# Attention on paired 64-row halves: masks, scores and maxima as 64-row products, tile-wise maxima five quarters ahead, four heads on two zero-interleaved copies

## The chip, the cores and the metric

One core of a Trainium2 chip. The metric is the device time of one execution in microseconds, lower is better. A comparison comes as a ratio of medians with a 95% interval.

## What is computed

A network of four blocks over x of shape (16, 256, 128) in f32, each with a residual and a layer norm ahead of it: a long convolution, a mixture of experts, attention, and the same mixture of experts again.

```
x = x + conv(norm(x))
x = x + ffn(norm(x))       # 8 experts, top 2, and a shared one, hidden width 512
x = x + attention(norm(x)) # 16 heads of width 8, 256 positions, ALiBi, causal
x = x + ffn(norm(x))       # the same weights
```

The attention is `softmax(q k^T / sqrt(8) + slope_h * (j - i), masked to j <= i) v`, then a product with Wout. The change lies in this block alone, and in the routing of the second expert block that is interleaved with it.

## The kernel before, in words

`build` runs four stages, one after the other, with a barrier between: `front_stage` (convolution, shared expert, routing of the first expert block), `attention_stage`, `shared_stage` (shared expert, rest of the routing of the second block) and `last_stage` (its routed experts, output). `attention_stage` (from L1662) begins with the routed experts of the first block (`routed_program`) and their sum and norm in five pieces (`middle_program`), then does attention batch by batch: 16 batches of 256 tokens, two tiles of 128 tokens each, and the 16 heads as four quarters `G` of four heads `g`.

Precision is made by splitting: a value is an f16 high part and an f16 low part. `project` (L1820) multiplies by the q and k weights, `highs` (L2002, ACT) and `split` (L2095, DVE) form the two parts, `store_qk` (L2008, three DMAs on ACT's queue) writes them to DRAM, and `load_qk` (L1758, five DMAs on SP's queue) brings them back as `KST` (128 rows: part, dimension, head of the quarter) and `QPAD`, in which head g has its values in rows g, g+4, ... and zeros in the others, so that a 128-row product with `KST` yields one head.

A batch has two halves of work, each once a quarter:

- `maxima` (L1838): the scores once with queries in the partitions, so that `reduce` (L2101, DVE, L2109) can take each query's maximum. Three blocks of 512 columns a quarter go alternately to banks 2 and 3; each begins with a product that adds the causal mask (L1845, L1851), then come the heads' products (L1847, L1855). Block n waits until block n-2 is reduced. After two quarters `split_maxima` (DVE), `turn_maxima` (PE, L1863), `maxima_rows` (ACT, L2026) and `spread_m` (L1767, four DMAs on SP's queue) put the negative maxima in two rows of `QPAD`, so that the next product subtracts them.
- `scores` (L1867): the scores again with keys in the partitions, into banks 5 to 7: three mask products (L1876, L1879) and three real ones (L1877, L1880). `expo` (L2028, ACT, L2031) takes the exponential of all 1536 columns at once; `weigh` (L1883, PE, L1894 and L1895) multiplies by v and a column of ones, in four tiles of 32 columns.

The rest of a batch: `take_out` (ACT, L2035), `turn_back` (PE, L1906), `normalise` (DVE, L2123 and L2125), `turn_out` (L1912), `out_high` and `out_low` (ACT L2040, DVE L2136), `project_out` (L1920), `add` (DVE, L2140), `statistics` (DVE, L2131). The norm ahead of the last block follows at once (`batch_norm_program`): `gpsimd` (POOL, L1050 to L1063), `scalar` (ACT, L1070), `turn` (two transposing DMAs on SP's queue, L1079). Three groups of four batches are also routed here: `gate` and `rank` on PE, `logits`, `largest`, `second`, `chosen`, `positions`, `place` on DVE, and the dispatch of two groups, eight tiles at a time, on POOL (L999, L1012).

Every engine runs an order written out by hand: in iteration b the maxima of batch b+1 (`first`), the scores and weighing of batch b (`second`), the projection of batch b+2 and the output of batch b-1, `for G in range(HG)`. On PE a quarter reads:

```
scores(b, q, G)
maxima(b + 1, 1 - q, G, (0, 1))
project(b + 2)              # G == 0
maxima(b + 1, 1 - q, G, (2,))
turn_back / turn_out / project_out of b - 1
weigh(b, q, G)              # waits for this quarter's exponential
values(b + 1)               # G == 3
```

## Time and profile before

| | |
|---|---|
| Median of 3 runs | 952.41 us (949.72 to 954.01) |
| Profiled execution | 951.15 us, its span 949.3 us |
| PE busy | 671.7 us, 71% of the span |
| PE weight loads | 491.6 us, 52% |
| DVE busy | 646.1 us, 68% |
| ACT busy | 445.5 us, 47% |
| POOL busy | 460.9 us, 49% |
| Mean granted TensorE clock | 0.890 of full speed |

The span runs from the first to the last instruction; the execution's own time is a little longer. An engine's busy time leaves out its waits and its register, branch, semaphore and DMA-issuing work. Products on PE are pipelined, so that records overlap: the distance from start to start tells more than a duration. The attention proper lies between about 407 and 735 us; the routed experts before and behind it have limits of their own. A wait is counted for the engine that stood idle and given to what ended it. SPq is SP's queue of DMA issues, ACTq that of ACT, PEld the weight loads.

### The profile page before, as it was taken

What the parts mean: (1) busy time and instruction counts of PE and PEld (TensorE: products, weight loads), DVE (VectorE), ACT (ScalarE), POOL (GpSimd) and SP (SyncE); (2) the same over time, 40 slices, a digit from 0 to 9 for tenths busy, and PEclk for the clock granted to TensorE, in tenths of its full rate; (3) what the DMA queues carried; (4) which work ended last, traced back from release to release, by engine and by line L of the source; (5) the groups of instructions that cost most, each with busy time, mean ns of one, the idle gap of its engine ahead of it and who ended that gap; (6) DMA issues with size and microseconds to landing.
All of it is one profiled execution on the core that took longest, in us unless ns stands there. A gap on an engine that the chain in (4) does not pass through costs nothing. (4 is left out here: it accounts for less than half of the span.)

```text
span 949.3 us, 21195 instructions
## 1 busy us (share of the span) xinstructions
PE 671.7 (71%) x7378; PEld 491.6 (52%) x7378; DVE 646.1 (68%) x1459; ACT 445.5 (47%) x873; POOL 460.9 (49%) x569
## 2 busy tenths in 40 slices
PE   0278964860099997157988988888983785999960
PEld 0163433650089996034555655555552464899850
DVE  6989987760278886685666676576661673788865
ACT  6632366730055554355455555455542431555534
POOL 2037758887537777110111226316421784477770
PEclk9978997985589999568999999999997897999995
DMA  9410002241444542521122223213300141454417
GB/s 288 109 35 1 0 7 70 66 88 52 40 73 91 98 92 44 199 57 41 41 66 63 55 63 86 80 52 90 86 8 12 43 80 31 81 96 93 96 32 265
DMA packets 137507, 70.45 MB, mean 74 GB/s; under 512 B 89237, under 2 KB 126619, under 8 KB 137400
## 3 DMA queue, kind: packets, MB, share of 16 engines
q1 hardware_dynamic: 113646, 44.16, 20.7%
q0 software_dynamic: 9088, 16.88, 6.1%
q10 hardware_dynamic: 14672, 8.06, 3.1%
q8 instruction: 64, 1.05, 0.5%
q14 instruction: 37, 0.30, 0.1%
HBM read 26.61 MB, written 30.50 MB: 60 GB/s over the span
## 5 line engine op out<-in xcount | busy, mean ns | idle before, releaser
L2109 DVE TENSOR_REDUCE ARENA<-banks 128x2 f32<-128x512 f32 (+1 forms) x192 | 126.8, 687 | 88.2 <-PE banks L1847 85.7
L1432 ACT ACTIVATE ARENA<-banks,ARENA 128x256 f32<-128x256 f32 x312 | 122.1, 475 | 109.7 <-PE banks L1395 97.6
L1393 PE MATMUL banks<-ARENA,W1H 128*128 128x256 f16 x312 | 87.2, 279 | 69.0 <-DMA ARENA<-slots 62.1
L2031 ACT ACTIVATE ARENA<-banks 128x1536 f32<-128x1536 f32 x64 | 92.0, 1437 | 58.7 <-PE banks L1880 58.7
L1407 PE MATMUL banks<-W2L,ARENA 128*128 x624 | 110.6, 219 | 2.7 <-DVE ARENA L1445 2.3
L1408 PE MATMUL banks<-W2H,ARENA 128*128 x624 | 110.0, 219 | 0.1
L1409 PE MATMUL banks<-W2H,ARENA 128*128 x624 | 110.1, 219 | 0.0
L1383 POOL DMA_INDIRECT expert_out_g<-ARENA x78 | 80.6, 1033 | 47.7 <-issue 25.8
L1383 POOL DMA_INDIRECT expert_out_f<-ARENA x78 | 81.3, 1043 | 39.0 <-issue 25.6
L1466 DVE TENSOR_TENSOR ARENA<-ARENA 128x1024 f16<-128x1024 f32 x78 | 95.6, 1226 | 2.7
L999 POOL DMA_INDIRECT slots<-ARENA,PLACE x64 | 77.3, 1208 | 26.1 <-issue 18.1
L1394 PE MATMUL banks<-ARENA,W1H 128*128 128x256 f16 x312 | 87.1, 279 | 0.0
L1395 PE MATMUL banks<-ARENA,W1L 128*128 128x256 f16 x312 | 87.0, 279 | 0.0
L1012 POOL DMA_INDIRECT slots<-ARENA,PLACE x64 | 77.5, 1210 | 19.1 <-issue 14.6
L1464 DVE CAST ARENA<-ARENA 128x1024 f16<-128x1024 f32 x78 | 58.2, 746 | 38.8 <-ACT ARENA L1432 34.2
L1393 PEld LDWEIGHTS banks<-ARENA,W1H 128*128 x312 | 31.2, 100 | 74.5 <-issue 70.9
L479 PE MATMUL banks<-XN,ARENA 128*128 128x512 f32 x64 | 32.2, 661 | 47.0 <-ACT XN L398 40.8
L1407 PEld LDWEIGHTS banks<-W2L,ARENA 128*128 128x128 f16 x624 | 60.9, 98 | 5.0 <-issue 3.9
L1408 PEld LDWEIGHTS banks<-W2H,ARENA 128*128 128x128 f16 x624 | 60.9, 98 | 1.6 <-issue 0.3
L1409 PEld LDWEIGHTS banks<-W2H,ARENA 128*128 128x128 f16 x624 | 61.0, 98 | 0.0
L1050 POOL TENSOR_TENSOR NRM<-RSTATS 128x2 f32<-128x2 f32 x15 | 3.1, 203 | 116.3 <-DVE RSTATS L2131 116.2
L1851 PE MATMUL banks<-ARENA 128*128 128x256 bf16 x128 | 36.3, 283 | 28.2 <-DVE ARENA L2109 28.0
(318 smaller groups left out, 1897.8 us busy)
## 6 DMA issues: line engine op xcount, KB each, us to landing
spread<-ARENA ACTq DMA_DIRECT2D x48, 128.0 KB, 2.0
ARENA<-expert_out_f SPq DMA_DIRECT2D x8, 512.0 KB, 7.2
ARENA<-spread SPq DMA_DIRECT2D x16, 256.0 KB
ARENA<-spread SPq DMA_DIRECT2D x64, 64.0 KB
ARENA<-expert_out_g SPq DMA_DIRECT2D x8, 512.0 KB, 7.2
XT<-in_w SPq DMA_DIRECT2D x10, 256.0 KB, 7.6
slots<-EMPTY SPq DMA_DIRECT2D x16, 129.0 KB, 4.7
ARENA<-in_w SPq DMA_DIRECT2D x8, 256.0 KB, 6.9
```

The costliest lines, as they stand in the source:

```text
L1012: nc.gpsimd.indirect_dma_start(xs, bass.IndirectOffsetOnAxis(ap=t.PLACE[:, 1, i:i + 1], axis=0), ROWI[:, i, :], None).then_inc(sent[h], 16)
L1383: nc.gpsimd.indirect_dma_start(yo, bass.IndirectOffsetOnAxis(ap=target, axis=0), Y[i % 4][:, h], None, bounds_check=2 * NT * P - 1, oob_is ...
L1393: pe.matmul(out, t.W1H[:, e, ms], XST[i][:, 0], start=True, stop=False)
L1394: pe.matmul(out, t.W1H[:, e, ms], XST[i][:, 1], start=False, stop=False)
L1395: ins = pe.matmul(out, t.W1L[:, e, ms], XST[i][:, 0], start=False, stop=True)
L1407: pe.matmul(out, hh, t.W2L[:, e, m, :], start=(m == 0), stop=False)
L1408: pe.matmul(out, hh, t.W2H[:, e, m, :], start=False, stop=False)
L1409: ins = pe.matmul(out, hl, t.W2H[:, e, m, :], start=False, stop=(m == MT - 1))
L1432: ins = nc.scalar.activation(HF[i % 2][:, m], UP[i % 2][:, m], ACT.Gelu, bias=BIAS[i % 4][:, m:m + 1], scale=1.0 / WS)
L1466: dve.tensor_tensor(H16[i % 4][:, 1], HF[i % 2], H16[i % 4][:, 0], ALU.subtract).then_inc(split, 1)
L2031: nc.scalar.activation(PR[G % 2], t.psum_all[:, 5:8, :], ACT.Exp, scale=1.0 / LOGIT).then_inc(exps, 1)
L2109: dve.tensor_reduce(out, src, AX.X, ALU.max).then_inc(m_red, 1)
```

## The change

All in `attention_stage` and `batch_norm_program`, with the layout of two host tables.

- Layout. The four heads of a quarter become two halves `a` of 64 partitions with two heads `s` each. `KST` keeps 128 rows, ordered half, dimension, part, head. `QPAD` has two copies `s` instead of four `g`: copy s has its heads' rows in every second partition and zeros between. A head's product now uses the 64 partitions of its half, in `KST` and `QPAD` alike.
- Masks. Instead of a 128-row identity times a mask there is a shifted identity `SPREAD` of 64 rows in each half and two masks, `LATER` and `EARLIER`; each mask is made by two products, one of the full 128 columns a head and one of 64.
- `maxima(y, tile)`: two calls a quarter, one for each query tile, half a into bank 2+a: mask products of 256 and 128 columns in each half, then for both heads 128 columns (tile 0) or 256 (tile 1), 16 products a quarter for 15. `reduce(y, tile)` takes both banks at once: 512 elements (tile 0) or 1024 (tile 1). Tile 0 is done four quarters ahead of the scores, tile 1 five.
- `scores(x)`: 12 products for 6, alternating between the halves; three semaphore steps instead of one, the middle of it with a wait, because half 1 writes to bank 7 after half 0.
- Order on PE: `maxima(x + 4, 0)`, `scores(x)`, `maxima(x + 5, 1)`, the batch's other work, and `weigh(x - 1)`, the weighing of the quarter before.
- The batch's other work moves: projection three batches ahead, output two batches behind, values into bank 0 at G = 2; turning back at G = 2 and 3, turning out at G = 0 and projecting out at G = 1 of the next iteration.
- DMAs. The stores of q and k go from ACT's queue (three) to SP's (six); the loads are three instead of five, and the maxima's rows two for each half batch instead of four. SP waits for batch b-3's rows between the two `spread_m` of batch b+1.
- Norm and routing. POOL's `gpsimd` is cut into `statistics(c)` and `rows(c)`, and the rows come one batch later, behind the next batch's statistics; ACT's part is one iteration later, gate and rank two iterations later, at G = 2; POOL dispatches four tiles at a time.
- The loops run from b = -2 to 17 instead of -1 to 16, and PE does `project(0)` ahead of them.

The diff, cut to its core:

```diff
-        QPAD = [carve(F16, HG, GH, SEQ) for _ in range(3)]
+        QPAD = [carve(F16, 2, HG, SEQ) for _ in range(3)]
         V32 = [carve(F32, TPB, NH, 32) for _ in range(2)]
-        IDB, MASKB, MASKT = carve(BF16, P), carve(BF16, GH, P), carve(BF16, GH, P)
+        SPREAD = carve(BF16, 2 * P)
+        LATER, EARLIER = carve(BF16, 2, P + HALF), carve(BF16, 2, 2 * P)
...
+            for b in range(-3, NB + 2):
+                if batch(b + 2):
                     load_qk(b + 2)
-            body(-2, 0, STAGES[-2])
-            pipeline(sp, body)
+                if batch(b + 3):
+                    store_qk(b + 3)
+                if batch(b + 1):
+                    spread_m(b + 1, 0)
+                if 0 <= b - 3 < NB - 1:
+                    batches.turn(sp, b - 3)
...
+                batches.statistics(pool, c)
+                if c >= 1:
+                    batches.rows(pool, c - 1)
+                for g in range(SENT_IN_ATTENTION):
+                    piece = c - 4 * g - 6
+                    if piece in (0, 1):
+                        route.dispatch_first(pool, g, range(GRP // 2 * piece, GRP // 2 * piece + GRP // 2))
+                    if piece in (2, 3):
+                        route.dispatch_second(pool, g, (piece - 2,))
...
+            def mask_later(out, a, part, start):
+                first, n = ((HALF + HALF * a, HALF), (HALF * a, P))[part]
+                rows = SPREAD[PAIR[a], first:first + P]
+                pe.matmul(out, rows, LATER[PAIR[a], :, first:first + n], start=start, stop=False, skip_group_check=True)
...
+            def maxima(y, tile):
+                c, G = divmod(y, HG)
+                if G == 0 and tile == 1:
+                    pe.wait_ge(qk_in[c % 3], 48 * (c // 3 + 1))
+                after(pe, m_red, 2 * y + 1 - tile)
+                keys, queries = P * tile + P, slice(P * tile, P * tile + P)
+                out = [ps[2 + a][:, 0:2 * keys].rearrange("p (s n) -> p s n", n=keys) for a in range(2)]
+                for a in range(2):
+                    mask_earlier(out[a][:, :, P * tile:P * tile + P], a, 0, True)
+                for a in range(2):
+                    mask_earlier(out[a][:, :, P * tile + HALF:P * tile + P], a, 1, False)
+                for s in range(2):
+                    for a in range(2):
+                        ins = pe.matmul(out[a][:, s], QPAD[c % 3][PAIR[a], s, G, queries], KST[c % 3][PAIR[a], G, 0:keys],
+                                        start=False, stop=True, skip_group_check=True)
+                        if s == 1:
+                            ins.then_inc(m_mm, 1)
...
+            def scores(x):
+                c, G = divmod(x, HG)
                 if G % 2 == 0:
-                    after(pe, mrow_in[G // 2], 64 * b + 64)
-                if b == 0 and G == 0:
...
+                after(pe, exps, x)
...
+                mask_later(late[0], 0, 1, True)
+                mask_later(early[1], 1, 1, True)
+                mask_later(late[0][:, :, 0:HALF], 0, 0, False)
+                mask_later(early[1][:, :, 0:HALF], 1, 0, False)
+                late_scores(0).then_inc(st_mm, 1)
+                early_scores(1)
+                mask_later(early[0], 0, 1, True)
+                mask_later(early[0][:, :, 0:HALF], 0, 0, False)
+                pe.wait_ge(st_mm, 3 * x + 1)
+                mask_later(late[1], 1, 1, True)
+                early_scores(0).then_inc(st_mm, 1)
+                mask_later(late[1][:, :, 0:HALF], 1, 0, False)
+                late_scores(1).then_inc(st_mm, 1)
...
+            def quarter_of(b, G):
+                x = HG * b + G
+                if quarter(x + 4):
+                    maxima(x + 4, 0)
+                if quarter(x):
+                    scores(x)
+                if quarter(x + 5):
+                    maxima(x + 5, 1)
+                if G == 0:
+                    if batch(b + 3):
+                        project(b + 3)
+                    if batch(b - 2):
+                        turn_out(b - 2)
...
+                if quarter(x - 1):
+                    weigh(x - 1)
...
+            def reduce(y, tile):
+                c, G = divmod(y, HG)
+                dve.wait_ge(m_mm, 4 * y + 4 - 2 * tile)
+                keys = P * tile + P
+                src = t.psum_all[:, 2:4, 0:2 * keys].rearrange("p a (s n) -> p a s n", n=keys)
+                dve.tensor_reduce(MX[:, G // 2, tile, :, :, G % 2].rearrange("p s a -> p a s"), src, AX.X, ALU.max).then_inc(m_red, 1)
...
+            def quarter_of(b, G):
+                x = HG * b + G
+                if quarter(x + 4):
+                    reduce(x + 4, 0)
+                    if G % 2 == 1:
+                        split_maxima(b + 1, G // 2)
+                if G == 1 and batch(b - 2):
+                    out_low(b - 2)
+                if quarter(x + 5):
+                    reduce(x + 5, 1)
+                if G == 0:
+                    if batch(b + 3):
+                        split(b + 3)
+                    if rank_group(b) is not None:
+                        route.second(dve, rank_group(b))
+                if G == 1:
+                    if batch(b - 2):
+                        add(b - 2)
+                    if rank_group(b) is not None:
+                        route.chosen(dve, rank_group(b))
+                if G == 2:
+                    if batch(b - 1):
+                        normalise(b - 1, 0)
+                    if batch(b - 2):
+                        statistics(b - 2)
+                    if gate_group(b) is not None:
                         route.logits(dve, gate_group(b), ps[0])
...
```

## Rows read from the trace of the kernel before

**Rows 1.** The exponential's line: durations, first and last start in us.
```profile
L2031 ACT ACTIVATE ARENA<-banks x64: 1422/1450/1452, 429.0 to 718.2; 128x1536 f32<-128x1536 f32 x64
```

**Rows 2.** Stretches of the attention stage: PE, PEld, DVE, ACT, POOL busy (x), clock.
```profile
400.00:429.00 29.00, 15.48 (x96) 9.89 (x97) 23.22 (x71) 15.05 (x42) 3.27 (x2) 0.62 0.23 63
...
521.50:540.00 18.50, 16.45 (x195) 10.56 (x188) 11.65 (x27) 9.52 (x13) 3.67 (x13) 1.00 0.24 66
540.00:558.40 18.40, 16.34 (x208) 10.64 (x201) 13.91 (x39) 9.51 (x13) 3.66 (x13) 1.00 0.23 63
```

**Rows 3.** Waits from 429 to 718: us in total, times, longest.
```profile
DVE ARENA L2109 <- PE banks L1847: 84.8, 57, 3.2
...
ACT ARENA L2031 <- PE banks L1880: 56.8, 32, 2.6
...
PE banks L1851 <- DVE ARENA L2109: 22.4, 46, 1.8
```

**Rows 4.** Timeline of PE in one quarter: start, us, instruction, wait ahead.
```profile
545.66 0.28 PE L1876 MATMUL banks<-ARENA 128*128 128x256 bf16 x1
...
547.20 0.27 PE L1851 MATMUL banks<-ARENA 128*128 128x256 bf16 x1
...
548.24 0.28 PE L1851 MATMUL banks<-ARENA 128*128 128x256 bf16 x1 [0.55 <-DVE ARENA L2109]
...
548.58 0.60 PE L1906 MATMUL banks<-ID,ARENA 128*128 128x128 f32 x4
549.12 0.66 PE L1894 MATMUL banks<-ARENA 128*32 128x256 f32 x8
549.57 0.42 PE L1895 MATMUL banks<-ARENA 128*32 128x128 f32 x8
549.93 0.28 PE L1876 MATMUL banks<-ARENA 128*128 128x256 bf16 x1
```

**Rows 5.** Groups by form, 429 to 718: busy us and mean ns behind the bar.
```profile
L2109 DVE TENSOR_REDUCE ARENA<-banks 128x2 f32<-128x512 f32 x120 | 82.3, 686 | 0.9 <-PE banks L1855 0.3
L1855 PE MATMUL banks<-ARENA 128*128 128x128 f16 x480 | 46.6, 220 | 0.0
L1877 PE MATMUL banks<-ARENA 128*128 128x512 f16 x126 | 44.9, 383 | 0.0
```

**Rows 6.** Timeline of the gate's weight loads, three to a token tile.
```profile
540.28 0.12 PEld L928 LDWEIGHTS banks<-GWH,XT 128*128 128x128 f16 x2
...
540.35 0.12 PEld L928 LDWEIGHTS banks<-GWH,XT 128*128 128x128 f16 x2
```

**Rows 7.** Timeline ahead of the first exponential, at 429.0.
```profile
402.27 2.62 SPq L1764 DMA_DIRECT2D ARENA<-spread  x4
...
406.71 0.59 PE L1845 MATMUL banks<-ARENA 128*128 128x512 bf16 x1 [4.26 <-DMA ARENA<-spread]
...
410.74 0.57 ACT L2005 ACTIVATE ARENA<-banks 128x512 f16<-128x512 f32 x1
...
422.85 1.23 DVE L1598 TENSOR_TENSOR RES<-RES,ARENA 128x1024 f32<-128x1024 f32 x1
```

**Rows 8.** Timeline of SP's queue over one batch.
```profile
568.80 2.50 SPq L1079 DMA_TRANSPOSE XT<-ARENA  x2
571.34 2.55 SPq L1770 DMA_DIRECT2D ARENA<-ARENA  x4
...
587.29 2.58 SPq L1079 DMA_TRANSPOSE XT<-ARENA  x2
```

**Rows 9.** Timeline behind the last exponential, batch 14's rows.
```profile
714.46 12.97 SPq L1079 DMA_TRANSPOSE XT<-ARENA  x4
...
719.62 0.20 POOL L1050 TENSOR_TENSOR NRM<-RSTATS 128x2 f32<-128x2 f32 x1 [5.23 <-DVE RSTATS L2131]
...
722.82 0.88 ACT L1070 ACTIVATE XN<-RES,NRM 128x128 f32<-128x128 f32 x2 [1.55 <-POOL NRM L1060]
...
724.25 0.65 POOL L1063 TENSOR_TENSOR ARENA<-XN,ARENA 128x256 f16<-128x256 f32 x1
```

More of the change, by code:

```diff
@@ L66 @@
 BACK_WORDS = 2 * NT * D
+HALF = P // 2
 class Bag:
@@ L1083, in landed @@
         eng.wait_ge(turned[(c - first) % 4], 16 * TPB * ((c - first) // 4 + 1))
-    part.gpsimd, part.scalar, part.turn, part.landed = gpsimd, scalar, turn, landed
+    part.statistics, part.rows, part.scalar, part.turn, part.landed = statistics, rows, scalar, turn, landed
     return part
@@ L1711, in attention_stage @@
         ps = t.psum
+        PAIR = [slice(HALF * a, HALF * a + HALF) for a in range(2)]
+        MAX_ROW = 30
+        LAST = HG * NB
         (consts_in, cleared, masks, cast, m_high, rc_set) = (sem(n) for n in (
@@ L1723, in after @@
         def after(eng, s, n):
-            if not (isinstance(n, int) and n <= 0):
+            if n > 0:
                 eng.wait_ge(s, n)
@@ L1754, in _, with store_qk @@
             sp.wait_ge(cleared, 8)
+            def store_qk(c):
+                after(sp, qk_in[c % 3], 48 * (c // 3))
+                sp.wait_ge(parts, c + 1)
+                words = DENSE[c % 2].rearrange("p k n -> p (k n)").bitcast(F32).rearrange("p (k n) -> p k n", k=4)
+                for i, kinds in enumerate(((1, 2), (1, 3), (0, 2))):
+                    for k in range(2):
+                        to = t.dram["spread"][c % 3][k][:, :, :, i].rearrange("s a d G n -> (s a d) G n")
+                        sp.dma_start(to, words[:, kinds[k]]).then_inc(dense_out[c % 2], 16)
@@ L1763, in load_qk @@
-                for g in range(GH):
-                    sp.dma_start(QPAD[c % 3][g:P:GH, :, g, :].bitcast(F32), q[g]).then_inc(qk_in[c % 3], 16)
-            def spread_m(c, r, h):
-                after(sp, mrow_set, 2 * c + h + 1)
-                for g in range(GH):
-                    row = GH * 26 + g
-                    sp.dma_start(QPAD[c % 3][row:row + GH + 1:GH, 2 * h:2 * h + 2, g, :],
-                                 MROW[h][4 * g:4 * g + 4, :]).then_inc(mrow_in[h], 16)
-            def body(b, q, stages):
-                second, first, projections, output = stages
-                if second:
-                    spread_m(b, q, 1)
-                if 2 <= b <= NB:
-                    sp.wait_ge(v_mm, b - 1)
-                    batches.turn(sp, b - 2)
-                if first:
-                    spread_m(b + 1, 1 - q, 0)
-                if projections:
-                    load_qk(b + 2)
@@ L1820, in project @@
             def project(c):
-                if c < TPB:
-                    pe.wait_ge(middle.low, 1)
+                if c <= 2 * TPB:
+                    pe.wait_ge(middle.low, c // TPB + 1 if c < 2 * TPB else NG)
+                after(pe, parts, c)
+                after(pe, mrow_set, 2 * (c - 2))
                 for k in range(2):
@@ L1972, in body @@
                         route.rank(pe, rank_group(b), ps[0])
-                    if b == 0:
-                        middle.turn(pe, 4 + G)
-                    if first and G == HG - 1:
-                        after(pe, added, b)
-                        if b == 0:
-                            pe.wait_ge(middle.low, NG)
-                        values(b + 1)
+                if G == 3:
+                    if batch(b + 1):
+                        after(pe, vset, b + 2)
+                        if gate_group(b) is not None:
+                            route.logits_taken(pe, gate_group(b))
+                        if rank_group(b) is not None:
+                            route.ranks_taken(pe, rank_group(b))
+                        turn_maxima(b + 1, 1)
+                    if batch(b - 1):
+                        turn_back(b - 1, 1)
@@ L1988, in _ @@
+            for b in range(-2, NB + 2):
+                for G in range(HG):
+                    quarter_of(b, G)
         @block.scalar
@@ L2077, in _ @@
             middle.normal(act, 2)
-            pipeline(act, body)
+            for b in range(-2, NB + 2):
+                for G in range(HG):
+                    quarter_of(b, G)
         @block.vector
@@ L2194, in _ @@
             middle.add(dve, 3)
-            pipeline(dve, body)
+            for b in range(-2, NB + 2):
+                for G in range(HG):
+                    quarter_of(b, G)
 def host_tables():
```

460 lines of the change are left out of this document (198 added, 262 removed).

## The prediction

> **What bounds the kernel now.** I read the stretches of the attention stage first, then the exponential's own rows, the waits, one quarter of a batch on PE, and last the two ends of the stage. From the first exponential (429.0) to the last (718.2) there are 63 intervals in 289.2 us [rows 1]; two batches' transposes on SP are 18.49 us apart, so a full quarter (one group G of one batch) takes 4.62 us [rows 8]. In such a batch PE is busy 16.4 of 18.5 us, DVE 11.7 to 13.9, ACT 9.5 [rows 2]. DVE's idle time ends with the first product of maxima, ACT's with the last product of scores; PE itself waits for one thing of weight, DVE's maxima, before it may write a bank again [rows 3]. So PE in program order is the bound, with a stall inside.
>
> A quarter on PE, start to start [rows 4]: scores and maxima block 0 1.54 (3584 columns at 2.4 per ns are 1.49), block 1 with the stall 1.04 (0.32 of it work, 0.72 stall), block 2 0.34, turning back 0.54 (0.44 plus 0.10 until the weighing starts), weighing 0.81. Without the batch's own work this is 3.90 with 0.17 for the drain ahead of the weighing: 1.54+1.04+0.34+0.17+0.81. The batch's own work is, by columns, project 0.64, turn out 0.22, two turned maxima 0.44, project out 0.32, turning back 0.88, values 0.32: 2.8 us. Four quarters plus that: 15.6+2.8 = 18.4 against 18.49 measured. The accounting holds, so I use it for the changed kernel.
>
> **Columns.** A 512-column product takes 383 ns and a 128-column one 220 ns [rows 5]: 384 columns in 163 ns, 2.4 columns per ns, plus 0.17 us until the result is there. Masks, scores and maxima stream 5120 columns a quarter now: 2.13 us. After: tile 0 of the maxima has 640 columns in each 64-row half, tile 1 has 896, the scores 1536. If the two halves run side by side that is 3072 columns, 1.28 us, and offsets in the scores (1640 by the order written) make it 1.32. The number of weight loads rises from 21 to 28 a quarter; load and 8-column product together follow at 25 ns here (three of each in 0.07 us) [rows 6], so 28 loads are 0.7 us and stay covered by the columns.
>
> Whether 64-row halves overlap no row shows. The nearest is the weighing, where four tiles of 32 columns take turns: eight products of 256 columns start within 0.45 us (549.12 to 549.57) [rows 4], where one after another they would need 0.85. Full overlap is one bound (1.32), none the other (6144 columns, 2.56 us). I take full overlap with 0.1 us lost, since that row is the nearest and shows tiles of one array overlapping.
> Going from the whole array to the 32-column tiles and back costs PE about 0.17 us before the weighing (its first product waits until the last result is out) and 0.20 behind it, the latter inside the 0.81 [rows 4]. The stretch of halves adds one such change a quarter, priced at the same 0.17 us; bounds 0 and 0.3.
> The Trainium skill ("TensorEngine Tiling (Array Packing)", Tiling Modes) has both rules: two 64x128 tiles load and multiply in parallel, and a change of tiling mode drains the engine. The trace agrees on the drain, with those 0.17 and 0.20 us; of 64-row tiles it shows nothing.
>
> **DVE.** Three reductions of 512 elements at 0.686 us [rows 5] become one of 512 and one of 1024; a 1024-element operation takes 1.23 us [rows 7]. 2.06 becomes 1.92 us a quarter. The new order decides more: maxima tile 0 is issued first, its reduction runs from 0.48 to 1.17 us in the quarter while the scores stream to 0.95, so the second maxima start at 1.22 instead of waiting 0.72. A stall of about 0.25 stays. Before, weighing waited for its own quarter's exponential; now it is the previous one's, which is done at 2.6 us.
>
> **The new quarter:** to the end of the second maxima 1.59 (1.22+0.37), switch 0.17, own work 0.71, drain 0.17, weighing 0.81: 3.45. With maxima turned behind DVE (0.2 in two quarters of four) 3.5 us; ACT (2.5 us of work) and DVE (about 3.0) fit beside it. I add 0.1 for pairs that do not line up and 0.1 for DVE's and ACT's fixed orders: **3.7 us**. 59 full quarters (all but the last four): 218.3 against 272.6 now.
>
> **Routing.** Three times, gate and ranking now stand at G=2 behind the values' evacuation (ACT does it after that quarter's exponential, so it is ready at about 3.1 us, and PE is there at 2.6), and largest, second and place are DVE work of 2.3 us a batch (13.91 against 11.65) [rows 2], which is free today. With DVE at 90% it isn't: I price 4 us a group, **12 us**, bounds 0 and 16.
>
> **The last four quarters** have no maxima: scores 0.68, switch 0.17, own work 0.71, drain 0.17, weighing 0.81, with waits 2.8 us each, 11.2 together, against 289.2-272.6 = 16.6 now.
> Stage between the exponentials: 218.3+12+11.2 = 241.5 against 289.2, **-47.7**.
>
> **Fill, +8.** Today the first maxima start at 406.7, ahead of the second projection's evacuation (410.74) [rows 7]; the first exponential at 429.0. Afterwards DVE's split of batch 1, which needs that evacuation, stands ahead of the first reduction in DVE's order, so the first reduction falls from 407.8 to about 412; a chain follows in which each tile's maxima wait for the other tile's reduction, partly at the low clock (0.62 in this stretch [rows 2]). Counted through in DVE's order, with about 0.9 us of PE between two reductions: the first three reductions end at 413.2, 414.8 and 417.1; batch 2's split at 418.4; the statistics of the expert output's fourth piece at 420.9; two reductions, the split maxima and the two low parts at 425.2; two more reductions at 428.2; that piece's weighting and addition (2.2 and 1.23 us) at 431.8; the last two at 434.7; then the scores at 1.2 GHz. First exponential near 437. Bounds +3 and +10.
>
> **Tail, +5.** Batch 14's statistics start POOL's chain at 719.62, at the end of the last exponential (718.2+1.45). POOL takes 3.2 us, ACT's two rows 0.88, POOL's two casts to 724.90, and the transposes' issue goes on to 727.43 (714.46+12.97) [rows 9]. After the change these statistics stand on DVE behind batch 15's first normalisation, which needs weighing (0.9), take-out (0.6) and turning back (0.7) before its own 0.55, all with their hand-overs; with the statistics' 0.5 that is 3.6 us after that exponential's end. POOL's chain ends at 6.9, and batch 13's rows, which moved behind it, at 8.0; batch 14's own follow at 9.2. So four transposes (1.25 us each) queue from 8.0 on: the last issue ends 13.0 us after the exponential instead of 7.8. Bounds +2 and +7.
>
> SP takes over six stores (ACT's three issues, about 0.45 us each, leave ACT), but has two loads and four spreads fewer: some 9 us of issue a batch, within 14. The memsets shrink by about 3 us, under the expert rounds: nothing.
>
> **Sum:** 951.15 - 47.7 + 8 + 5.2 = 916.7. The profiled execution is 1.3 us below the median of 952.41, so **917.5** as a median. A measurement tells about 0.5% (4.8 us) from nothing.
>
> **Rivals.**
> (1) *A chain over SP becomes the bound.* The row statistics of batch b-2, POOL's sums and rows (4.6 us: 719.62 to 724.90 [rows 9], less ACT's 0.88, with a wait), two transposes (2.5), then on the same queue the second half of the maxima's rows (2 of the 0.64 us issues: 2.55 for four [rows 8]) and some 1.8 us of landing (issue over at 404.9, PE off at 406.71 [rows 7]) must be over before the scores of G=2 in the next batch. From those scores to the statistics' end it is 3.9 us by the new quarter's count. The ring is 3.9+4.6+2.5+1.3+1.8, 14.1 us in all, beside PE's 14.0 to 14.8 a batch. For it: everything sits behind SP's wait for rows. Against: 14.1 us is still within four quarters of 3.7. With 1.8 us of contention the quarter is 4.0: 59 x 4.0+12+11 = 259, time 934. Chance 0.20.
> (2) *The stalls I priced do not come:* quarter 3.5, routing 4, fill 4: 206.5+4+11 = 221.5, time 893. Chance 0.12.
> (3) *The halves do not overlap*, so the change does not do what its pairing says. Stretch 2.56 instead of 1.59; the quarter is 2.56+0.17+0.71+0.17+0.81 = 4.4, with waits 4.5: 265.5+4+12.4 = 282, time 951-7+13 = 957: slower. It decides once stretches exceed 2.4 us. For it: twelve score products where there were six, and no 64-row form in the trace. Against: the weighing's overlap. Chance 0.06.
> By the Trainium skill ("TensorE: Matmul & The Clock Gate", Measured speedup vs the span model) four row tiles gave 3.07 times; an estimate at that 77% efficiency makes the stretch's columns 1.67 us, about 0.3 us a quarter above mine, 935 in all; no run here shows it yet.
> (4) *The granted clock falls to 1.2 GHz*, as it stood for part of 400 to 429 [rows 2], since PE waits elsewhere more. The 2.7 us of columns in a quarter double: 59 x 2.6 more, about 1070. Against: at 16.4 of 18.5 us busy it stands at 1.00, and PE would still be busy three quarters of the time; 0.02.
>
> **Numbers.** The forecast has 0.60, its own range 903 to 930. The range holds it, rival 1 and the nearer part of rival 2: 897 to 938. Faster 0.91 (forecast, rivals 1, 2 less a rest), same 0.03, slower 0.06.
>
> **What the profile would show.** Products of form 64*128, two starting within a few ns in different halves; a stretch of about 1.6 us; reductions of 1.22 us for 1024 elements; exponentials 3.6 to 3.8 apart; first exponential near 437; last transpose 13 us behind the last exponential. I am wrong if pairs start one after the other, if exponentials wait for the DMA of maxima rows, or if DVE is busy through and PE waits for it.

## The result, and the profile after

| | before | after |
|---|---|---|
| median of 6 runs, us | 952.07 (949.72 to 954.01) | 901.90 (899.87 to 902.89) |
| profiled execution, us | 951.15, span 949.3 | 901.03, span 899.3 |
| TensorE's granted clock, mean | 0.890 | 0.876 |
| ratio | | 0.9474 (0.9456 to 0.9492) |

The change takes 50 us where 34.5 were forecast. By the marks that the prediction set in the stage, the two spans differ so:

| stretch | before | after | difference | forecast |
|---|---|---|---|---|
| start of the program to start of the attention stage | 250.1 | 250.5 | +0.4 | 0 |
| from there to the experts' first product | 11.2 | 5.7 | -5.5 | 0 |
| from there to the first exponential | 167.7 | 174.2 | +6.5 | +8 |
| first to last exponential | 289.2 | 230.6 | -58.7 | -47.7 |
| last exponential's start to the next stage | 17.3 | 24.6 | +7.3 | +5.2 |
| behind it | 213.8 | 213.8 | 0 | 0 |

The differences sum to -50.0 (each was taken before rounding). The page's head and first part after:

```profile
span 899.3 us, 21979 instructions
PE 633.2 (70%) x7826; PEld 468.5 (52%) x7826; DVE 635.0 (71%) x1395; ACT 445.1 (49%) x873; POOL 456.7 (51%) x569
```

The exponential's line, which answers to [rows 1]:

```profile
L2072 ACT ACTIVATE ARENA<-banks x64: 1422/1450/1452, 430.3 to 660.9; 128x1536 f32<-128x1536 f32 x64
```

The same 64 instructions of 1.45 us, the first 1.4 us later, the last 57.3 earlier. Stretches of the stage, as in [rows 2]:

```profile
445.00:500.00 55.00, 53.20 (x824) 34.95 (x824) 43.20 (x80) 36.40 (x48) 6.77 (x27) 1.00 0.25 70
500.00:560.00 60.00, 54.33 (x857) 36.00 (x857) 46.16 (x100) 37.50 (x52) 14.50 (x53) 1.00 0.27 76
```

PE is the bound as before, at a granted clock of 1.00 (2.4 GHz): 53.2 of 55 us busy in the quiet batches (those without routing). DVE went up to 79% (43.2 of 55). The waits from 430 to 661, against [rows 3]:

```profile
ACT ARENA L2072 <- PE banks L1919: 58.2, 62, 3.2
DVE ARENA L2150 <- PE banks L1891: 40.3, 75, 1.9
PEld banks L1875 <- DVE ARENA L2150: 27.0, 71, 3.6
```

ACT and DVE wait for PE's products. PE's own wait for the maxima is still there, in the smaller form that the prediction left it. The quarter on PE, start to start, against [rows 4]:

```profile
542.82 0.34 PE L1875 MATMUL banks<-ARENA 64*128 64x256 bf16 x4
543.00 0.28 PE L1891 MATMUL banks<-ARENA 64*128 64x128 f16 x4
543.11 0.33 PE L1868 MATMUL banks<-ARENA 64*128 64x256 bf16 x4
...
543.78 0.27 PE L1919 MATMUL banks<-ARENA 64*128 64x256 f16 x1
544.18 0.34 PE L1875 MATMUL banks<-ARENA 64*128 64x256 bf16 x4
544.35 0.40 PE L1891 MATMUL banks<-ARENA 64*128 64x256 f16 x4
544.67 0.28 PE L1899 MATMUL banks<-ID,ARENA 128*16 128x128 f16 x2
544.88 0.65 PE L1960 MATMUL banks<-ID,ARENA 128*128 128x128 f32 x4
545.47 0.66 PE L1948 MATMUL banks<-ARENA 128*32 128x256 f32 x8
545.92 0.42 PE L1949 MATMUL banks<-ARENA 128*32 128x128 f32 x8
546.28 0.34 PE L1875 MATMUL banks<-ARENA 64*128 64x256 bf16 x4
```

Three things are to be seen. The maxima of tile 0, 1280 columns of both halves together (L1875 masks, L1891 products), go from 542.82 to 543.11: 4.4 columns per ns, where the whole array took 2.4 in the kernel before. The scores' 3072 columns follow from 543.11 to 543.89, 0.78 us or 3.9 columns per ns; their last 256-column product starts at 543.78. And the stall that was 0.72 us is now 0.29: from 543.89, 0.11 us behind that start, to tile 1's start at 544.18. The whole quarter is 3.46 us. The reductions, against [rows 5], have the two forms that were priced, at 1.23 and 0.69 us:

```profile
L2150 DVE TENSOR_REDUCE ARENA<-banks 128x4 f32<-128x1024 f32 x59 | 72.3, 1226 | 27.5 <-PE banks L1891 27.5
...
L2150 DVE TENSOR_REDUCE ARENA<-banks 128x4 f32<-128x512 f32 x59 | 40.8, 692 | 14.0 <-PE banks L1891 12.7
```

From the starts of the 64 exponentials: in batch 3 they stand 3.54, 3.27, 3.49 and 3.45 us apart, 13.75 a batch. Before, the shortest batches (1 and 2) had 4.02, 4.66, 3.78 and 4.93, 17.39 in all, and batches 3 and 4 took 17.9. Batch 0 takes 18.5 (24.8). The batches with routing take 15.2, 16.9 and 14.5 (7, 8, 9) and 15.0, 16.9 and 14.1 (11, 12, 13).

### The profile page after: what moved, and what is told of

It reads as the page before. It is cut to its first block and busy times, and to the rows that moved or that the text cites. A ratio compares the mean times of both kernels' runs of the same rounds, so it can differ in the third digit from the quotient of the medians.

```text
span 899.3 us, 21979 instructions
## 1 busy us (share of the span) xinstructions
PE 633.2 (70%) x7826; PEld 468.5 (52%) x7826; DVE 635.0 (71%) x1395; ACT 445.1 (49%) x873; POOL 456.7 (51%) x569
## 5 line engine op out<-in xcount | busy, mean ns | idle before, releaser
L2150 DVE TENSOR_REDUCE ARENA<-banks 128x4 f32<-128x1024 f32 (+1 forms) x128 | 122.7, 959 | 46.7 <-PE banks L1891 45.4
L1388 POOL DMA_INDIRECT expert_out_g<-ARENA x78 | 80.6, 1034 | 47.7 <-issue 25.8
L1875 PE MATMUL banks<-ARENA 64*128 64x256 bf16 (+1 forms) x512 | 45.6, 258 | 32.8 <-DVE ARENA L2150 23.6
```

The source lines that it names most:

```text
L1388: nc.gpsimd.indirect_dma_start(yo, bass.IndirectOffsetOnAxis(ap=target, axis=0), Y[i % 4][:, h], None, bounds_check=2 * NT * P - 1, oob_is ...
L2150: dve.tensor_reduce(MX[:, G // 2, tile, :, :, G % 2].rearrange("p s a -> p a s"), src, AX.X, ALU.max).then_inc(m_red, 1)
```

## Experiments

They ran in four sessions. In two of them the kernel before took 953 us, in the other two 1065 and 1054, one of these on a chip that had given 953 in another session; so each ratio is against the runs of before in its own session, and effects under 1% are read in traces, of which there is one for each kernel. The extra time is not in the quiet quarters, which keep 13.75 and 17.39 us a batch to 0.01 us. Between the exponentials of kernels of the before type it lies in batches 7, 8, 11 and 12, where POOL scatters rows; they go from about 18 to 26 us. That is 32 of the 114 us by which the profiled run with 2 KB rows (below) is longer than that of before. 10 us more lie ahead of the attention stage, 39 in its routed experts ahead of the first exponential, and 33 in the stages behind it. What makes a session long was not found.

### The order of issue: one half behind the other

In each of the three groups half 0's products are all issued ahead of half 1's:

```diff
-                for a in range(2):
-                    mask_earlier(out[a][:, :, P * tile:P * tile + P], a, 0, True)
-                for a in range(2):
-                    mask_earlier(out[a][:, :, P * tile + HALF:P * tile + P], a, 1, False)
-                for s in range(2):
-                    for a in range(2):
+                for a in range(2):
+                    mask_earlier(out[a][:, :, P * tile:P * tile + P], a, 0, True)
+                    mask_earlier(out[a][:, :, P * tile + HALF:P * tile + P], a, 1, False)
+                    for s in range(2):
```

> The changed kernel with the same 28 products a quarter, but all of half 0 issued before all of half 1, so that two halves meet only where one ends and the other begins. Theory P (the halves run side by side and that halves the stretch): the stretch grows from 1.6 to about 2.5 us, a quiet quarter from 3.44 to 4.3, exponentials' span from 230.6 to about 285, time 950 to 960, that is the time before the change. Rival O (the new order and the weighing a quarter late took the stalls away, PE has slack): a quarter grows by under 0.2 us, time under 915.

Measured: 903.9 us, ratio 0.9486 (0.9463 to 0.9509), a quiet batch of 13.88 us. Rival O's number came, but not for its reason: the pairs do not live by their order, and the timeline of PE (tile 0 of a quarter) says why:

```profile
544.42 0.35 PE L1875 MATMUL banks<-ARENA 64*128 64x256 bf16 x4
544.60 0.28 PE L1889 MATMUL banks<-ARENA 64*128 64x128 f16 x4
544.71 0.33 PE L1868 MATMUL banks<-ARENA 64*128 64x256 bf16 x2
```

All four masks start before any product of L1889, although half 0's two products stand in the program ahead of half 1's two masks; and tile 0 still takes 0.29 us (544.42 to 544.71). So products for the other rows of the array start ahead of earlier ones, and here the pairing did not need the order of issue. The run leaves the overlap as it was and so doesn't price it. That took two more.

### The overlap itself: the halves held apart, and its control

The first holds half 1 until half 0 is done, in each of the three groups; the second has as many new waits, behind both halves. In the first, the new wait inside the scores takes the place of the one that stood there.

```diff
                 for a in range(2):
+                    if a == 1:
+                        pe.wait_ge(m_mm, 4 * y + 3 - 2 * tile)
...
                 early_scores(0).then_inc(st_mm, 1)
+                pe.wait_ge(st_mm, 3 * x + 2)
                 mask_later(early[1], 1, 1, True)
```

```diff
                             ins.then_inc(m_mm, 1)
+                pe.wait_ge(m_mm, 4 * y + 4 - 2 * tile)
...
                 late_scores(1).then_inc(st_mm, 1)
+                pe.wait_ge(st_mm, 3 * x + 3)
```

> The kernel after, with the second half's products held back: in each of the three groups of a quarter's stretch (maxima of tile 0, scores, maxima of tile 1) PE waits for a semaphore that half 0's last product raises before it issues half 1's first. Theory P (two 64-row products run side by side, which is what the quarter lives on): the stretch's 6144 columns (1280, 3072 and 1792) then run at one column a cycle, 2.56 us at 2.4 GHz, where side by side they take 1.28; with three waits of some 0.2 us the quiet quarter goes from 3.45 to 5.0 to 5.4 us and the run to 990 to 1015 us. Rival O (the 0.29 us of a tile's starts is how the records come out, and the time is one of handovers): only the waits are paid, the quarter is about 4.0 us and the run about 940, like the run with waits alone.

> The control for the run with the halves held apart: the kernel after, with three waits a quarter as well, but behind both halves of a group (PE waits for the group's last product before it issues what follows), so that the halves still run side by side. Both theories: three waits of some 0.2 us each, a quiet quarter of about 4.0 us and a run of about 940 us. What the run with the halves apart costs above this one is the price of losing the overlap: 1.28 us a quarter, some 55 to 78 us in all, by theory P, under 10 us by rival O.

Measured: 972.4 us, ratio 1.0178 (1.0136 to 1.0219), with the halves apart; 924.5, ratio 0.9694 (0.9669 to 0.9718), with the waits alone. The quiet quarters are 4.55 and 3.84 us (18.18 and 15.37 a batch). So a wait costs 0.13 us on average (0.40 us for three), not 0.2, and holding the halves apart costs 0.70 us a quarter on top. In all that is 48 us: 42 between the exponentials, 5.5 ahead of the first and 1 behind the last. Rival O, which gave it less than 10, fell. Theory P gave 1.28 us a quarter, 55 to 78 in all, and is right in kind but too high. This kernel keeps some overlap between its groups, though how much of the missing 0.58 us that is was not measured. PE with the halves apart:

```profile
500.68 0.28 PE L1875 MATMUL banks<-ARENA 64*128 64x256 bf16 x1
500.74 0.27 PE L1868 MATMUL banks<-ARENA 64*128 64x256 bf16 x1
500.80 0.22 PE L1875 MATMUL banks<-ARENA 64*128 64x128 bf16 x1
500.85 0.21 PE L1868 MATMUL banks<-ARENA 64*128 64x128 bf16 x1
```

Half 1's masks for the scores (L1868) and half 0's for the next group, tile 1 (L1875), start in turns, 0.05 to 0.06 us apart. The 48 us thus price the overlap inside the groups, and are a lower bound for all of it. With 48 us more the changed kernel would stand at 950: an estimate, by which the overlap is worth as much as the whole gain. The parts need not add up, since the new order may gain nothing where the halves are slow; the joined reductions were not tried alone.

### The weighing a quarter later

```diff
-                if quarter(x - 1):
-                    weigh(x - 1)
+                if quarter(x):
+                    weigh(x)
```

with ACT's take-outs one quarter earlier.

> The changed kernel with each quarter's weighing in its own quarter again (as before the change), and the two copies of its result a quarter earlier. Theory W (with PE this fast its own exponential is not done yet): PE reaches the weighing 2.3 to 2.6 us into the quarter and the exponential ends at 2.65, so 0.1 to 0.4 us a quarter, time 909 to 920, and the wait of the weighing for the exponential rises from 1 to over 10 us. Rival S (the batch's own work covers it, as it did before): within 3 us of 902.

Measured: 911.1 us, ratio 0.9567 (0.9544 to 0.9590); a quiet batch of 14.3 to 14.5 us, about 3.6 a quarter. The weighing now waits for its own quarter's exponential:

```profile
500.90 0.66 PE L1948 MATMUL banks<-ARENA 128*32 128x256 f32 x8 [0.16 <-ACT ARENA L2072]
```

Moving the weighing behind by a quarter is worth 9 of the 50 us.

### The second maxima four quarters ahead, not five

```diff
-                if quarter(x + 5):
-                    maxima(x + 5, 1)
+                if quarter(x + 4):
+                    maxima(x + 4, 1)
```

DVE reduces in the same order, so that the split of the maxima (L2159) comes behind the long reduction.

> The changed kernel with both tiles of the maxima four quarters ahead (tile 0, scores, tile 1 of the same quarter), so that the maxima are split behind the long reduction. Theory L (the fifth quarter of lead takes the 1024-element reduction out of the way of PE's turned maxima): PE waits about 1.6 us in G=1 and G=3, a quiet batch grows from 13.75 to about 17 us, time 945 to 955, first exponential 1 to 3 us earlier. Rival N (DVE is not in the way, the lead only costs fill): time 898 to 903.

Measured: 987.7 us, ratio 1.0354 (1.0319 to 1.0389). That is 86 us above the changed kernel and beyond every expectation. The waits from 440 to 720:

```profile
PE banks L1899 <- DVE ARENA L2159: 51.3, 27, 2.3
ACT ARENA L2067 <- PE banks L1899: 39.7, 27, 2.7
```

The turning of the maxima (L1899) stands in the middle of PE's program, and its input is now made behind the long reduction, which itself waits for this quarter's second maxima. PE stands still for 1.9 us in every second quarter, ACT's copy of the turned rows waits behind it, and so do the exponentials. That is 51 of the 86 us, and about what theory L priced. Most of the rest goes with TensorE's granted clock. It is 0.84 over 440 to 560, where the changed kernel has 1.00 from 445 on, and it falls behind most of PE's stands:

```profile
508.29 0.27 PE L1899 MATMUL banks<-ID,ARENA 128*16 128x128 f16 x2 [1.86 <-DVE ARENA L2159]
...
509.53 1.10 PE L1948 MATMUL banks<-ARENA 128*32 128x256 f32 x8
...
511.00 0.50 PE L1875 MATMUL banks<-ARENA 64*128 64x256 bf16 x4
```

From 508.3 to 511.8 the granted clock was 0.52, that is the lower level of 1.2 GHz, and from 511.9 to 518 it was 1.00. The weighing takes 1.47 us start to start (509.53 to 511.00) instead of 0.81. By the trace's clock records there are 23 such stretches from 440 to 720 for 27 stands, 85 us in all. At half speed they cost PE at most 43 us, where 35 us lie beyond the waits; the split is an estimate, and no run held the clock apart from the waits. The fifth quarter of lead keeps DVE's chain out of PE's.

### The start of the stage: four runs

Here 5.5 us came that no term of the sum had. Two things differ there: POOL's clearing is shorter (8.2 us, now 5.6), and the fixed rows are copied in another form. The first run is the changed kernel with its three cleared copies cleared twice:

```diff
+            for v in words:
+                nc.gpsimd.memset(v, 0.0).then_inc(cleared, 1)
+            pool.wait_ge(cleared, 3)
             for v in (*words, V32[0], V32[1], SPREAD, LATER, EARLIER):
```

The others are the kernel before with its copies changed. First they are written as 2 KB rows:

```diff
-                sp.dma_start(t.dram["spread"][r][:, 3], t.dram["fixed_rows"]).then_inc(consts_in, 16)
+                sp.dma_start(t.dram["spread"][r][:, 3].rearrange("k d g G n -> k (d g) (G n)"),
+                             t.dram["fixed_rows"].rearrange("k d g G n -> k (d g) (G n)")).then_inc(consts_in, 16)
```

Then each is split into two that take every other row:

```diff
+                for g in range(2):
+                    sp.dma_start(t.dram["spread"][r][:, 3].rearrange("k d g G n -> k (d g) (G n)")[:, g::2],
+                                 t.dram["fixed_rows"].rearrange("k d g G n -> k (d g) (G n)")[:, g::2]).then_inc(consts_in, 16)
```

Last, the copies are turned so that the 32 rows are outermost:

```diff
+                sp.dma_start(t.dram["spread"][r][:, 3].rearrange("k d g G n -> (d g) k (G n)"),
+                             t.dram["fixed_rows"].rearrange("k d g G n -> (d g) k (G n)")).then_inc(consts_in, 16)
```

> The changed kernel with its three cleared copies cleared twice, so that POOL's clearing is as long as before the change (8.2 instead of 5.6 us) while the constant rows keep their new form. Theory M (POOL's clearing at the stage's start holds up DVE's copies and the first expert): first expert product 3 to 5 us later, time 905 to 907. Rival F (the form of the constant rows did it): 902, DVE's two copies longer but nothing behind them.

> The kernel before the change, with nothing altered but the form of its first three DMAs of the attention stage: the constant rows go as rows of 2 KB (as in the changed kernel) instead of as two stretches of 64 KB. Theory F (the long stretches hold up the DMA engines, and with them the first expert's transposed tile): the first expert product comes at 256 instead of 261.3 us, time about 5 us less, 947. Rival M (POOL's longer clearing holds it up): no change, 952.

> The kernel before, with each of the three copies of the fixed rows split into two that take every other 2 KB row, so that a copy can't be sent as two runs of 64 KB each. Theory R (the long runs hold up the transposes that stand behind them in the queue): the first expert's first product comes about 7.5 us behind the start of the clearing, where it is 11.1 now (5.7 as in the kernel after, and three more issues of 0.6 us), and the run is 3 to 4 us shorter, 948 to 949 on a chip where before takes 952. Rival C (it is the clearing or the placement of something else in that stage that the change altered): 11 to 13 us, and no gain, or 2 us of loss for the three more issues.

> The kernel before, with the same three copies of the fixed rows written with the 32 rows of 2 KB as the outer dimension and q against k inside, where before, and in the run that split them, q against k (two) is outermost. Theory E (a copy is dealt to the DMA engines by its outermost dimension, so that two of them carry all of it, and the transposes' packets stand behind): the copies land within 3 us, the first expert's first product comes 5.5 to 6 us behind the start of the clearing instead of 11.1, and the run is 5 to 5.5 us shorter: ratio 0.994 to 0.995. Rival N (something else of the changed layout, not these copies): 11 us as before and a ratio of 1.000.

Measured, from the start of the clearing to the experts' first product: before 11.2 us; after 5.7; clearing doubled 5.7 (ratio 0.9531, 0.9478 to 0.9584); 2 KB rows 11.1 (1.0016, 0.9967 to 1.0066); every other row 11.1 (0.9991, 0.9977 to 1.0005); rows outermost 5.7 (0.9927, 0.9888 to 0.9966). It is not the clearing, since doubling it changed nothing. Written as 2 KB rows the copies were sent as before: rows that lie next to each other in memory still went as six packets of 64 KB (3219 packets in that run's view, 3213 of them under 8 KB), so that run did not test the length. With every other row 192 packets of 2 KB went, and the first product came no sooner (its three more issues put the transposes back by 1.9 us only), so it is not the length either. The DMA view of the stage's first microseconds (busy tenths of the 16 engines in 40 slices) before, 249 to 262:

```profile
DMA  0000000090000000009999900440000000799992
...
DMA packets 2327, 0.79 MB, mean 61 GB/s; under 512 B 2321, under 2 KB 2321, under 8 KB 2321
```

(The time of a packet counts in the slice in which it starts: the 9 alone in its place is the first two 64 KB packets, of 3.3 to 3.5 us each.)

With every other row in a copy, 249 to 264:

```profile
DMA  0000000011120111111011699971411999912087
```

With the rows outermost, 250 to 270:

```profile
DMA  0000000355730560247025620661183208411008
...
spread<-in_fixed_rows SPq DMA_DIRECT2D x3, 128.0 KB, 2.6
```

With q against k, two, as the outermost dimension and every other row in a copy, a tenth to two tenths of the engines are busy for some 4 us, about two of 16. The packet records say the same: before, two of the six 64 KB packets are under way at a time, and the last ends at 260.06, ahead of the experts' first product at 261.3. With 32 rows outermost up to 19 packets of 2 KB are under way at once, the copies land in 2.6 us, and the transposes behind them in the same queue bring the experts their rows 5.4 us sooner. That the outermost dimension deals a copy out to the engines is the reading that fits all six kernels; no record here names the engine of a packet. The Trainium skill has it as a rule ("DMA: Bandwidth & Descriptors", Why a DMA increments its semaphore by 16 and not by 1): the largest number up to 16 that divides the slowest dimension of both sides, so two engines for the old form and 16 for 32 or 64 rows. The trace agrees, with two packets at a time for the old form, and with 11.1 us against 5.7. The changed layout puts 64 rows outermost, so the 5.5 us come with it by the way, and the kernel before can have them by changing one statement (measured in the long session, 0.7% with an interval of 0.3 to 1.1).

### Routing behind the weighing

In the quarter G = 2 of the changed kernel the gate's products and the ranks' stand ahead of the weighing and wait there for ACT's evacuation of the values (here the gate's):

```profile
541.34 0.19 PE L929 MATMUL banks<-GWH,XT 128*128 128x8 f16 x2 [0.67 <-ACT ARENA L2061]
```

The edit moves both blocks, unchanged, behind `weigh(x - 1)`. It ran in two sessions.

> The changed kernel with gate and rank behind the weighing at G=2 instead of ahead of it. Theory G (PE stands 0.7 us for ACT's copy of the values and then does the gate, with everything behind it late): the long quarters at G=2 of the routing batches (4.9 us) shrink by 0.5 to 1.0 us, six of them, time 897 to 900. Rival D (DVE's routing work sets those quarters): no change, 901 to 903.

> The kernel after, with the gate's products and the ranks' issued behind the quarter's weighing instead of ahead of it, on the chip of the first runs. By the intervals seen on the other chip (the third quarter of a gate's batch 4.18 us instead of 4.91, of a rank's 3.81 instead of 4.36, the batch of the first transposes behind it 14.3 instead of 15.2) it gains 2 to 3 us in all: some 899 us, ratio 0.944 to 0.945. If the routing's cost is all in DVE's work and PE's place doesn't matter: 902, ratio 0.947.

Measured: ratios 0.9460 (0.9407 to 0.9513) and 0.9480 (0.9425 to 0.9534), against 0.9474 for the change. In the intervals the gate's quarter falls from 4.91 to 4.18 us and the ranks' from 4.36 to 3.81, in both sessions. With 0.2 us lost elsewhere in the ranks' batch (16.6 against 16.9) this is 1 us a group, less than both expectations had. The times can't show so little: both sessions were those of the long batches. Most of what is left of the ranks' batch (16.6 against 13.75) is in its first two quarters, 4.7 and 4.6 us, where PE waits for DVE, which then does the routing's arithmetic as well. In the changed kernel it waits 0.95 us at 548.45, and then:

```profile
553.32 0.34 PE L1875 MATMUL banks<-ARENA 64*128 64x256 bf16 x4 [1.37 <-DVE ARENA L2150]
```

### The tail

```diff
-                pool.wait_ge(row_stats, c + 1)
-                batches.statistics(pool, c)
                 if c >= 1:
                     batches.rows(pool, c - 1)
+                pool.wait_ge(row_stats, c + 1)
+                batches.statistics(pool, c)
```

and DVE's statistics of batch b - 2 ahead of the normalisation of b - 1.

> The changed kernel with POOL's rows of batch c-1 ahead of its statistics of batch c again, and DVE's statistics at G=2 ahead of the normalisation. Theory T (the end of the stage is the chain statistics of batch 14, POOL, ACT, POOL, four transposes queued): the last transposes are issued 2 to 4 us earlier after the last exponential, the next stage begins as much earlier, time 898 to 900. Rival B (the barrier or batch 15 sets the end): 901 to 903.

Measured: ratio 0.9466 (0.9421 to 0.9512), and 24.1 us from the last exponential's start to the next stage, against 24.6. DVE's statistics do come sooner (4.7 us behind the exponential's end instead of 6.2), but POOL begins on them 6.8 us behind it, as against 7.0. It now stands at batch 13's row first:

```profile
738.38 0.40 POOL L1067 CAST ARENA<-XN 128x256 f16<-128x256 f32 x1 [2.38 <-ACT XN L1075]
...
739.60 0.20 POOL L1052 TENSOR_TENSOR NRM<-RSTATS 128x2 f32<-128x2 f32 x1
```

What DVE's half of the edit gave, POOL's half mostly took back. Statistics moved alone were not tried.

## Why the prediction was right, and where it was not

The median, 901.9, lies in the range, and 1 us under the low end of the forecast's own, which had the chance of 0.60. The mechanism is the one that was named, and the sizes of five steps were off. From 917.5 to 901.9 are -15.6 us: -11 between the exponentials, -5.5 at the start of the stage, -1.5 in the fill, +2.1 in the tail and 0.4 ahead of the stage. Without the 5.5 us, which no term had, the run would have stood near 907, inside the forecast's own range.

**The quarter.** Counted from the columns it was 3.45 us, and 3.44 was measured. The parts agree too: from tile 0's start to tile 1's 1.27 to 1.36 us for 1.22, from there to the weighing 1.34 on average for 1.42, the weighing 0.81 for 0.81. Then 0.05 for turned maxima and 0.2 for pairs that do not line up and for fixed orders were put on top, up to 3.7, with no row behind the 0.2. (0.2 in two quarters of four are 0.1 and not 0.05, so the sum as written gives 3.75.) Over 59 quarters the 0.26 are 15.3 us, the largest part of the miss. The scores did take 0.78 us for 0.68, but PE waits there for the reduction of tile 0 in any case, the order of issue changed only 2 us in all, and DVE, at 79%, had room.

That the same accounting seemed to hold for the kernel before was luck. It gave 18.4 us a batch and was held against 18.49, the distance of two batches' transposes on SP; the shortest batches take 17.39. It counted a stall of 0.72 us in all four quarters, but at G = 0 the projection (L1827, 454.13 to 454.78) stands in its place; the wait is seen in the quarter behind it:

```profile
454.13 0.38 PE L1827 MATMUL banks<-XT,QKWH 128*128 128x256 f16 x2
...
458.94 0.28 PE L1851 MATMUL banks<-ARENA 128*128 128x256 bf16 x1 [0.45 <-DVE ARENA L2109]
```

Over 59 intervals the 4.62 us hold (272.6 for 273.3) because the first batch and the routing are in them.

**Batch 0** was in the old sum, inside 289.2, but not in the new one: 59 equal quarters leave out that the first batch runs 4.8 us over the others. **The last four** quarters took 12.2 us, not 11.2; a wait for a row of the maxima, 1.5 us at 657.04, stands in them. **Routing** was priced at 12, for three groups. The 59 intervals sum to 218.35; less 59 x 3.44 (203.0) and batch 0's 4.8, that leaves 10.6, of which 10.0 lie in the six batches named above. The sum held by luck: only two groups' gates and ranks fall into these intervals (541.3 and 601.6; the third gate is at 658.4), at 5 us each and not 4. DVE was 81% busy in a ranks' batch (13.7 of 16.9 us), not 90. "Free today" was wrong too: before, batches 5 and 6, 9 and 10, 13 and 14 already ran 0.9 to 2.2 us over a quiet one. Together: -15.3 + 4.8 + 1.0 - 1.4 gives the -11 between 241.5 and 230.6. (The last sum has a slip as well: 916.7 and 1.3 are 918.)

**The start of the stage** was taken as nothing: "the memsets shrink by about 3 us, under the expert rounds". For the memsets that is right, and the doubled clearing shows it. What was missed stands one line above in SP's order: three copies whose form changed, with the experts' transposes queued behind them. That is 5.5 us.

**Fill and tail.** +6.5 for +8, inside the bounds, and by the way that was named. The first reduction stands behind DVE's split of batch 1 (L2142), which waits for ACT's evacuation:

```profile
405.00 0.69 DVE L2142 TENSOR_TENSOR ARENA<-banks,ARENA 128x512 f16<-128x512 f32 x1 [2.76 <-ACT ARENA L2057]
405.61 1.22 DVE L2150 TENSOR_REDUCE ARENA<-banks 128x4 f32<-128x1024 f32 x1
```

Its 405.6 is not to be held against 412, since everything here comes 5.1 us earlier. From the experts' first product it is 149.5 us, before 146.5: 3.0 later, where 4.2 were forecast. The chain behind it, the alternation of reductions and maxima, took 3.5 more, where 3.8 were. The tail's +7.3 for +5.2 is past its upper bound. The working stopped at batch 15's normalisation; ahead of batch 14's statistics DVE also had the last group's routing to do:

```profile
663.31 0.70 DVE L968 SCALAR_TENSOR_TENSOR ARENA<-ARENA 128x64 f32<-128x64 f32 x1
...
668.56 0.48 DVE L2172 BATCH_NORM_STATS2 RSTATS<-RES 128x6 f32<-128x128 f32 x2
```

so the last transpose was issued 16.4 us behind the exponential instead of 13.0:

```profile
663.96 14.82 SPq L1084 DMA_TRANSPOSE XT<-ARENA  x6
```

**The rivals.** SP's ring (1) did not bind, but it was near: scores waited twice for a row, 2.8 us in all, once in the last four quarters (above), and once in batch 4, which became 1.5 us longer by it:

```profile
504.08 0.34 PE L1868 MATMUL banks<-ARENA 64*128 64x256 bf16 x4 [1.30 <-DMA ARENA<-ARENA]
```

(2), no stalls, was right on the quarter and wrong on routing (4 for 10) and on the fill (4 for 6.5). (3) fell with 4.4 columns per ns. Its price was fair: with the 48 us, the run would be at 950 with part of the overlap left, and the rival said 957 with none. (4) fell for this kernel: the granted clock stood at 1.00 from 445 to 661. With one quarter of lead less it came in part. The 3.07 times (77%) of four row tiles that the Trainium skill gives ("TensorE: Matmul & The Clock Gate", Measured speedup vs the span model) would have meant 935, by the prediction's estimate. With two tiles here the maxima of tile 0 ran at 92% (4.4 of 4.8 columns per ns) and the scores at 82% (3.9), and part of that was covered by PE's wait for the reduction.

## What to carry to other kernels

Check a count from columns and hand-overs on a single quiet batch of the old loop, not on a distance that has other work in it; once it holds there, let it stand for the new loop, for a margin belongs in the range, not in the sum. Look at each DMA whose layout changes, even a constant's, and at what is queued behind it: a copy with an outermost dimension of two held a stage up by 5.4 us. And when work is moved ahead in time, ask which engine's last product of the quarter feeds another's middle, for there one quarter of lead was worth 86 us, 51 of them waits, and most of the rest, by the estimate above, a lower clock behind the waits.

## What the runs showed of the hardware

- Products in two 64-row halves of the array run side by side (1280 columns in 0.29 us, 4.4 per ns, where the whole array took 2.4), and one half's products can start ahead of the other half's earlier ones (masks at 544.42 to 544.55, products from 544.60). Where a semaphore orders the halves, products of the next group still start between those of the held half, 0.05 to 0.06 us apart.
- A wait of PE for its own last product, with the change of stream behind it, costs 0.13 us (three of them 0.40 us a quarter).
- Behind a stand of 1.9 us PE's granted clock was 0.52 from 508.3 to 511.8, and the same weighing took 1.47 us instead of 0.81.
- Three copies of 128 KB between places in memory kept two packets of 64 KB under way with two as the outermost dimension, and up to 19 packets of 2 KB with 32; the transposes queued behind them served the experts 5.4 us sooner.
- The same chip gave 953 and 1054 us for the same kernel in two sessions. Quiet batches kept their length to 0.01 us; batches 7, 8, 11 and 12 of the before type, with POOL's scatters, grew by 8 us or more each.
